# The last slots of a pipelined cross-attention kernel in another order

## The reference, cut to what matters

```
a = layer_norm(ctx) * gamma + beta
Q, K, V = x @ Wq.T, a @ Wk.T, a @ Wv.T        # split into 16 heads
scores = einsum('bhtd,bhsd->bhts', Q, K) * scale, masked
attn = softmax(scores, axis=-1)               # exp(s - max) / sum
out = einsum('bhts,bhsd->bhtd', attn, V)      # heads joined again
return x + tanh(gate) * (out @ Wo.T)
```

## Time and profile before

| what | value |
|---|---|
| runs of the kernel before | 990.89, 991.29, 989.62 us; median 990.89 |
| the profiled execution's own time | 989.58 us |
| its span | 987.4 us |
| TensorE busy over the span | 965.6 us, 98% |
| VectorE busy | 793.3 us, 80% |
| ScalarE busy | 691.8 us, 70% |
| GpSimd busy | 607.4 us, 62% |
| mean granted clock of TensorE | 0.989 of full speed |

### The profile page before, as it was taken

The page is one execution under the profiler, slowest core; times in us unless marked ns, Lnnn a source line. Parts: engine busy times, 40 slices in busy tenths (PEclk is TensorE's granted clock), DMA queues, the critical chain, the costliest instruction groups (busy, mean ns, idle before and its releaser), DMA issues.

```text
span 987.4 us, 29829 instructions
## 1 busy us (share of the span) xinstructions
PE 965.6 (98%) x10655; PEld 805.7 (82%) x10655; DVE 793.3 (80%) x1446; ACT 691.8 (70%) x1364; POOL 607.4 (62%) x731
## 2 busy tenths in 40 slices
PE   9999999999999999999999999999999999999965
PEld 8899888888888888888888888888888888888853
DVE  6961688888898888888888888888888888888776
ACT  3422778777777777777777777777777777777662
POOL 0952466666766666667667666666666676766534
PEclk9999999999999999999999999999999999999987
DMA  9741333333332333333333233333333332331111
GB/s 294 228 122 32 77 81 76 96 99 96 91 83 75 85 97 88 88 90 95 98 87 94 77 81 88 97 79 96 90 95 97 87 94 74 85 86 37 26 37 41
DMA packets 80019, 89.86 MB, mean 91 GB/s; under 512 B 21888, under 2 KB 58752, under 8 KB 79968
## 3 DMA queue, kind: packets, MB, share of 16 engines
q10 hardware_dynamic: 29311, 46.24, 18.7%
q1 hardware_dynamic: 50657, 42.93, 15.9%
HBM read 79.05 MB, written 10.09 MB: 90 GB/s over the span
## 4 chain that ended last, share of the span: by engine, by line
PE 92%; DVE 2%; DMA 2%; POOL 2%; ACT 1%; issue 0%; ACTq 0%; SPq 0%; DVEq 0%; POOLq 0%
PE bank L861 65%; PE sbank L999 11%; PE bank L1015 9%; PE bank L884 3%; PE bank L1021 2%; PE sbank L884 2%; DMA qT<-in_wvT 1%; POOL gbo L421 1%; ACT shared_f L624 1%; PE bank L984 1%; POOL xy L425 0%; ACT shared_f L588 0%; DMA qT<-in_wqT 0%; DVE shared_f L810 0%; DVE shared_f L808 0%
## 5 line engine op out<-in xcount | busy, mean ns | idle before, releaser
L778 DVE TRANSPOSE_TENSOR_REDUCE rmax<-shared_f 128x14 f32<-128x448 f32 x384 | 230.5, 633 | 91.0 <-ACT shared_f L588 82.0
L461 POOL TENSOR_TENSOR shared_f<-shared_f 125x448 f32<-125x448 f32 x128 | 150.1, 1173 | 245.3 <-ACT shared_f L624 243.2
L861 PE MATMUL bank<-shared_r,w_k 128*128 128x376 f32 x1536 | 298.5, 343 | 0.0
L861 PE MATMUL bank<-w_v,shared_r 128*125 128x512 f32 x1152 | 283.6, 395 | 0.0
L861 PEld LDWEIGHTS bank<-shared_r,w_k 128*128 128x128 f32 x1536 | 258.4, 188 | 21.5 <-issue 21.1
L588 ACT ACTIVATE shared_f<-sbank,mask_b,rstd 125x448 f32<-125x448 f32 x384 | 250.4, 723 | 25.6 <-PE sbank L999 25.5
L861 PEld LDWEIGHTS bank<-w_v,shared_r 128*125 128x125 f32 x1152 | 212.8, 186 | 44.8
L788 DVE TENSOR_TENSOR shared_f<-shared_f,bank 125x448 f32<-125x448 f32 x384 | 215.3, 616 | 4.4
L624 ACT ACTIVATE shared_f<-shared_f 125x448 f32<-125x448 f32 x384 | 194.5, 580 | 15.0 <-DVE shared_f L788 14.9
L465 POOL TENSOR_TENSOR shared_f<-shared_f 125x448 f32<-125x448 f32 x128 | 150.3, 1174 | 31.3 <-POOL shared_f L461 28.2
L659 ACT ACTIVATE shared_f<-bank,rstd 125x512 f32<-125x512 f32 x96 | 66.0, 688 | 132.4 <-PE bank L861 132.4
(11 more groups left out here) (93 smaller groups left out, 801.2 us busy)
## 6 DMA issues: line engine op xcount, KB each, us to landing
cn<-in_ctxT ACTq DMA_DIRECT2D x120, 187.5 KB, 2.4
rows<-in_ctx ACTq DMA_DIRECT2D x29, 720.0 KB
x<-row_stats SPq DMA_DIRECT2D x128, 84.0 KB
xy<-in_x SPq DMA_DIRECT2D x32, 224.0 KB, 3.1
out<-xy SPq DMA_DIRECT2D x32, 224.0 KB, 3.2
shared_f<-in_xT SPq DMA_DIRECT2D x7, 896.0 KB, 9.2
row_stats<-rmax SPq DMA_DIRECT2D x128, 21.0 KB
rows<-in_ctx SPq DMA_DIRECT2D x3, 720.0 KB
```

What stands on the lines that cost most here:

```text
L461: pool.tensor_tensor(psum[0:SP_, :], prob[0:SP_, q, 0, :], prob[0:SP_, q, 1, :], ALU.add).then_inc(sum_half, 1)
L778: last = dve.tensor_reduce(rmax[:, (r - 1) % 2, BLK * j:BLK * j + BLK], prob[:, (r - 1) % NB, j, :].rearrange("p (k a) -> p k a", a=32), A ...
L861: last = pe.matmul(dst, l, m, start=(start and k == 0), stop=(stop and k == len(pairs) - 1))
```

## The change

It touches only the slots from 128 on.

- GpSimd no longer sums chunks 125, 126 and 127. In `weighted_sum` these three (`late`) wait for each tile of exponentials by itself and form the denominators from the three tiles with twelve matmuls by ones, accumulated in PSUM.
- VectorE: slot 128 is quadrant maxima of chunk 127, low half of batch 30, maximum and subtraction of chunk 125. Slot 129: those of chunk 126. Slot 130: those of chunk 127, then `last_divide(0)` to `(2)`, `last_low(0)`, `last_low(1)`. Slot 131: `last_divide(3)`, `last_low(2)`, `last_low(3)`, `last_result`. `last_divide(3)` reads the numerators and denominators of chunk 127 from the PSUM bank.
- ScalarE: the high half of batch 30 moves ahead of the exponentials in slot 128, the gated output of batch 30 from slot 130 to the end of slot 129; chunk 127's bank isn't emptied by ScalarE; `last_high(2)` and `(3)` stand in slot 131.
- TensorE: the output of batch 30 moves from slot 129 to slot 128, ahead of the weighted sum of chunk 125. `last_output` waits for the high part of a chunk before its first pass, and for the low part only before its third.

```diff
 GpSimd, slot
-                if live(i, LOOP, r - 3, SLOTS):
+                if live(i, LOOP, r - 3, SLOTS - 3):
                     sum_chunks(i, r)
 ScalarE, slot (high_half and gated_out are the old lines as functions)
+                if is_slot(i, r, SLOTS):
+                    high_half(i, B - 2 - 2 * i)
                 if live(i, LOOP, r - 3, SLOTS):
...
-                if is_slot(i, r, SLOTS + 3):
-                    last_high(2)
-                if live(i, LOOP, r - 4, SLOTS):
+                if live(i, LOOP, r - 4, SLOTS - 1):
                     weighted_out(i, r)
...
                 if is_slot(i, r, SLOTS + 3):
+                    last_high(2)
                     last_high(3)
...
+                if u == 0 and whole(i, c - 2) and not is_slot(i, r, SLOTS):
+                    high_half(i, c - 2)
...
+                if u == 2 and whole(i, c - 2) and not is_slot(i, r, SLOTS + 2):
+                    gated_out(i, c - 2)
+                if is_slot(i, r, SLOTS + 1):
+                    gated_out(i, B - 2 - 2 * i)
 VectorE
             def last_divide(k):
-                dve.wait_ge(pv_out, SLOTS - KT + k + 1)
+
                 d = den[:, k * T:k * T + T]
-                dve.reciprocal(d, d).then_inc(last_step, 1)
+                if k < KT - 1:
+                    dve.wait_ge(pv_out, SLOTS - KT + k + 1)
+                    dve.reciprocal(d, d).then_inc(last_step, 1)
+                    o = last_chunk(k)
+                else:
+                    dve.wait_ge(pv_mm, SLOTS)
+                    dve.reciprocal(d, bank[PB][:, T:2 * T]).then_inc(last_step, 1)
+                    o = bank[PB][:, 0:T]
                 dve.wait_ge(last_step, k + 1)
-                dve.tensor_tensor(last_chunk(k), last_chunk(k), d, ALU.mult).then_inc(last_norm, 1)
+                dve.tensor_tensor(last_chunk(k), o, d, ALU.mult).then_inc(last_norm, 1)
...
                 if is_slot(i, r, SLOTS):
                     quadrant_maxima(i, r)
+                    low_half(i, B - 2 - 2 * i)
...
-                for k in range(KT):
-                    if is_slot(i, r, SLOTS + k):
-                        if k == KT - 1:
-                            for j in range(k):
-                                last_low(j)
-                        last_divide(k)
-                        if k == KT - 1:
-                            last_low(k)
-                            last_result()
+                if is_slot(i, r, SLOTS + 2):
+                    for k in range(KT - 1):
+                        last_divide(k)
+                    last_low(0)
+                    last_low(1)
+                if is_slot(i, r, SLOTS + 3):
+                    last_divide(3)
+                    last_low(2)
+                    last_low(3)
+                    last_result()
 TensorE, last_output
                 for k in range(KT):
-                    pe.wait_ge(last_done, k + 1)
                     for e, (a, d) in enumerate(PASSES):
+                        if e == 0:
+                            pe.wait_ge(last_hi, k + 1)
+                        if a == 1:
+                            pe.wait_ge(last_done, k + 1)
 TensorE, weighted_sum
-                pe.wait_ge(exp_done, i * (LOOP * ST) + (r - 2) * ST)
+                late = isinstance(i, int) and LOOP * i + r >= SLOTS
+                if not late:
+                    pe.wait_ge(exp_done, i * (LOOP * ST) + (r - 2) * ST)
                 for j in range(ST):
+                    if late:
+                        pe.wait_ge(exp_done, i * (LOOP * ST) + (r - 3) * ST + j + 1)
...
-                pe.wait_ge(sum_done, i * LOOP + (r - 2))
-                for h in range(HC):
-                    last = pe.matmul(bank[PB][HD * h:HD * h + HD, T:2 * T], ones[0:SP_, :],
-                                     psum[0:SP_, T * h:T * h + T], start=True, stop=True)
+                if not late:
+                    pe.wait_ge(sum_done, i * LOOP + (r - 2))
+
+                terms = [prob[:, (r - 3) % NB, j, :] for j in range(ST)] if late else [psum]
+                for j, term in enumerate(terms):
+                    for h in range(HC):
+                        last = pe.matmul(bank[PB][HD * h:HD * h + HD, T:2 * T], ones[0:SP_, :],
+                                         term[0:SP_, T * h:T * h + T],
+                                         start=(j == 0), stop=(j == len(terms) - 1))
 TensorE, slot
-                if is_slot(i, r, SLOTS + 1):
+                if is_slot(i, r, SLOTS):
                     output(i, r)
```

More of the change, by code:

```diff
@@ L591, in scores_out, with high_half, gated_out @@
                                    scale=rstd[0:SP_, c % 2, j:j + 1]).then_inc(s_out, 1)
+            def high_half(i, b):
+                act.wait_ge(o_norm, i * 2 + (b + 1))
+                if behind(i, 2, b):
+                    act.wait_ge(y_mm, i * 2 + b)
+                act.activation(oT[:, 0, :, :].rearrange("p c t -> p (c t)"),
+                               pv[:, b % 2 * HT:b % 2 * HT + HT], ACT.Copy).then_inc(o_hi, 1)
+            def gated_out(i, b):
+                act.wait_ge(y_mm, i * 2 + (b + 1))
+                if behind(i, 2, b):
+                    act.wait_ge(y_done, i * 2 + b)
+                act.activation(gated[0:T, :], bank[VO[0]][0:T, :], ACT.Copy, scale=gat[0:T, 0:1]) \
+                    .then_inc(y_out, 1)
             def last_high(k):
@@ L803, in normalise, with low_half @@
                 dve.tensor_tensor(o, o, spread, ALU.mult).then_inc(o_norm, 1)
+            def low_half(i, b):
+                dve.wait_ge(o_hi, i * 2 + (b + 1))
+                dve.tensor_tensor(oT[:, 1, :, :].rearrange("p c t -> p (c t)"),
+                                  pv[:, b % 2 * HT:b % 2 * HT + HT],
+                                  oT[:, 0, :, :].rearrange("p c t -> p (c t)").bitcast(F32),
+                                  ALU.subtract).then_inc(o_done, 1)
             def last_divide(k):
-                dve.wait_ge(pv_out, SLOTS - KT + k + 1)
                 d = den[:, k * T:k * T + T]
-                dve.reciprocal(d, d).then_inc(last_step, 1)
+                if k < KT - 1:
[6 more added lines that the diff above has]
+                    o = bank[PB][:, 0:T]
                 dve.wait_ge(last_step, k + 1)
-                dve.tensor_tensor(last_chunk(k), last_chunk(k), d, ALU.mult).then_inc(last_norm, 1)
+                dve.tensor_tensor(last_chunk(k), o, d, ALU.mult).then_inc(last_norm, 1)
             def last_low(k):
@@ L833, in slot @@
                     quadrant_maxima(i, r)
-                for k in range(KT):
-                    if is_slot(i, r, SLOTS + k):
-                        if k == KT - 1:
-                            for j in range(k):
-                                last_low(j)
-                        last_divide(k)
-                        if k == KT - 1:
-                            last_low(k)
-                            last_result()
+                if is_slot(i, r, SLOTS + 2):
+                    for k in range(KT - 1):
+                        last_divide(k)
+                    last_low(0)
[5 more added lines that the diff above has]
+                    last_result()
                 if u == 3 and whole(i, c - 1):
                     normalise(i, c - 1)
[L845 to L851, removed]
+                if u == 0 and whole(i, c - 2) and not is_slot(i, r, SLOTS):
+                    low_half(i, c - 2)
                 if u == 1 and live(i, 2, c + 2, B) and not first_two(i, c + 2):
@@ L1010, in weighted_sum @@
                     pe.wait_ge(v_done, i * (2 * ST) + (c + 1) * ST)
-                pe.wait_ge(exp_done, i * (LOOP * ST) + (r - 2) * ST)
+                late = isinstance(i, int) and LOOP * i + r >= SLOTS
+                if not late:
+                    pe.wait_ge(exp_done, i * (LOOP * ST) + (r - 2) * ST)
                 for j in range(ST):
+                    if late:
+                        pe.wait_ge(exp_done, i * (LOOP * ST) + (r - 3) * ST + j + 1)
                     for h in range(HC):
                         col = HD * (HC * u + h)
-                        pe.matmul(bank[PB][HD * h:HD * h + HD, 0:T],
+                        last = pe.matmul(bank[PB][HD * h:HD * h + HD, 0:T],
                                   v_sb[0:SP_, c % 2, j, col:col + HD],
```

## The result

| kernel | median | runs | lowest to highest |
|---|---|---|---|
| before | 990.87 us | 6 | 989.62 to 992.67 |
| changed | 986.58 us | 6 | 985.29 to 988.19 |

The ratio is 0.995, with a 95% interval of 0.9936 to 0.9964: 3.6 to 6.3 us faster, 4.3 by the medians. Forecast were 986.1 and a gain of 4.8.

A forecast was written before the change was run, and what follows sets the result against it. TensorE, busy 98%, was taken to bound the body, and chunk 127's chain and the last output the tail. Gains 3.6 + 0.65 + 0.6 = 4.85, say 4.8, against the median of 990.89 gave 986.1 us, range 983.9 to 988.3.

The forecast's parts named there:

- The place of the change: Slots from 128 on: only the tail changes; in the body, where TensorE is busy 98% of the time, nothing does.
- The low half: VectorE, batch 30, ahead of chunk 125's maximum: waits for GpSimd's add and ends at 960.3; by shared bandwidth 961.1.
- The maxima: VectorE, chunks 125 to 127: chunk 127's maximum starts at 968.15 instead of 971.73, gain 3.6 us.
- The denominators: TensorE, chunk 127's ones matmuls: last output 2.5 us behind the weighted sum's start instead of 3.15, gain 0.65.
- High parts first costs nothing.: TensorE, `last_output`: high parts before low ones move the needs later at no cost; could give back up to two matmuls.
- TensorE's queue: Batch 30's output ahead of chunk 125's sums: chunk 126's end at 970.9, ScalarE wants them at 971.5, 0.6 us cover.
- The last output's clock: TensorE, last output: high clock for some of the twelve matmuls, 0.6 us off the 5.19 at the low clock.
- The sum: Whole tail: 3.6 + 0.65 + 0.6 = 4.85 us gain, say 4.8; 986.1 us against the median.
- Rival 1: TensorE: high clock from chunk 127's sums on, matmuls then wait for VectorE; gain 5.6, 985.3 us; chance 0.15.
- slow transfers: Tail: both reads at 3.95 us, chunk 127's write may hold its read; gain 2.0, 988.9 us; chance 0.11.
- slower: Tail: reads and write of 5.6 us each put chunk 127's maximum 4.5 late; 991.2 or 993 us; chance 0.04, equal included.

The follow-up runs named there:

- the two with the output 2.5 us or more later: Against the changed kernel: output of batch 30 back in slot 129, tail 24.0 us; low half of batch 30 behind chunk 125's subtraction, tail 23.2 us.
- the two-buffer kernels: Changed kernel plus a second buffer for chunk 126's maxima: 983.87 us; that plus three edits of order (store, bias, low part 0): 981.98 us.

## Why the prediction was right, point by point

- **The place of the change.** That only the tail moves is borne out; from the first quadrant maxima to those of chunk 127 the two kernels take 856.1 to 856.8 us in four executions.
- **The low half.** Forecast +2.6 for the maximum of chunk 125, measured +2.4. GpSimd's add ran from 961.23 to 962.49 and the low half ended 0.48 behind it, 0.83 long; with no add beside it, it took 0.58 to 0.62 in three experiments. By a sharing of bandwidth I had priced 1.68. The rows before could have told the two apart, against what I wrote: there the add ended at 964.59 + 1.29 = 965.88 and the low half at 964.68 + 1.68 = 966.36, the same 0.48 behind it. In all nine executions in which the two overlap it is 0.47 to 0.49. I had read only the length. By the lock that the Trainium skill, "SBUF — State Buffer", section "SBUF: two separate sides", describes, both rows agree.
- **The maxima.** Gain forecast 3.6, measured 3.9. Putting two divisions back took 1.8 of it away; with GpSimd's sums back instead, the maximum stood at +10.6, 0.4 later. So the order of the work carries it, as forecast. That the read of `x4` would show next was right (1.29 and 0.82 us idle). How the 6.85 us were split was wrong: I gave 2.9 to the first and 3.95 to the second read, by their neighbours on the queue. They took 3.6 and 3.1, and turning the write round changed no more than reads differ by themselves. That two errors of 0.7 and 0.8 cancel in the sum is luck.
- **The denominators.** The term "the last output began 3.15 behind 975.47, now 2.5" had the size almost right (3.15 to 2.4) by luck, and the cause wrong. Before, the ones matmuls ended at 977.74, but the output waited until 978.62 for low part 0, itself behind a GpSimd add. The bracket of that row, 0.88 <-DVE L814, says so, against my sentence that the low parts did not hold the last output. The sums left on GpSimd cost about 1.9 us, through VectorE and the clock.
- **"High parts first costs nothing."** It costs nothing, but I took it as worth nothing as well, because VectorE's run was forecast at 975.4 against a need at 975.3. Waiting for the low part first cost 2.0 us beside the reads: 0.8 by the later start, some 0.5 by a collision that the edit does not cause, and 0.7 in the output's length.
- **TensorE's queue.** Chunk 126's sums ended at 972.1 and ScalarE came at 974.07, 1.9 us later, not 0.6: the clock had gone up within the output and the sums took 1.4 instead of 2.5. I had kept the low clock throughout.
- **The last output's clock.** Forecast 4.6, measured 4.25 and 4.40: the rise came within the last output, between the two cases that I had priced.
- **The sum.** 4.85 forecast for the tail, 5.5 measured: 0.3 more in the maxima, 0.1 in the denominators, 0.35 in the last output's length. The median, 986.58 against 986.1, came closer than this sum, and that is partly luck: the medians are 4.3 apart while the tails are 5.5 apart, and what lies between comes from the start, which no term covers. Rival 1, the high clock from chunk 127's sums on, did not come in this kernel (0.50 from 974 to 979), but it did in four of the variants. The rivals of slow transfers and of slower have no support: no read in the tail took over 3.9 us.

## What to carry to other kernels

Work that stands in an in-order queue ahead of the last item of a chain costs its own time and the waits that it brings; move it behind, then look at once for the transfer that it had hidden, and give that a second buffer. Where GpSimd and VectorE both read two SBUF operands, move GpSimd's work out of the critical stretch even if nobody waits for its result. Here a product of 112 columns took 0.27 us alone and up to 1.19 beside an add of 1.3, and putting the sums back cost 1.9 us, clock included, where the wait that one saw was 0.9. Compare such a change from a mark just ahead of the edited code, since a start that varies by 3 us hides half of a gain of 5.

## What the runs showed that I had not expected

The clock of the tail changes with what stood on TensorE before it. With the output of batch 30 started by +2.5 and two waits of 1.7 to 3.5 us behind it, chunk 127's 24 records took 1.35 in all six executions (five kernels) that have this. In four variants they took 0.78, and there the waits between the output and these records are 0.5 to 1.4 us: the two with the output 2.5 us or more later, and the two-buffer kernels, whose output is as early as in the changed kernel. In these four the last output went at the high level too, 1.00 in the stretch from 976 to 981 of one of them. So the output's place alone does not decide. What the two groups differ in is the length of the waits behind it, but no run changed only that. The kernel before stands between them: behind a wait of 3.35 its 24 records took 0.78, and the last output was at 0.50 again.

In matmul time the low level costs 1.1 us in the sums of chunk 127 and 0.9 in the last output. At the end of the changed kernel only about 1.0 of it can show (an estimate: low part 0 at +16.95, ten matmuls in 2.6 and 3.6 to the end of the span make 23.2, against 24.2). The experiment with the low half behind the subtraction came to just that. So doing one block early, with long waits behind it, can cost about 1 us at the end.
